# Half-width output matmuls in the first attention, and one probability tile normalised on the scalar engine

## What is computed

```python
x = LN(x + attention0(x))   # 16 heads of 8, differential: a = softmax(q1 k1) - lam * softmax(q2 k2), no mask
x = LN(x + ffn0(x))         # 352 wide, fp4 quantised inputs and weights, silu gate
x = LN(x + attention1(x))   # 16 query heads of 64, 4 key heads, rotary, causal softmax
x = LN(x + ffn1(x))         # 8 experts of 512, top 1, relu
```

```python
w = softmax(where(causal, q @ k.T / 8, -1e30)); out = w @ v
```

## Time and profile before

| | |
|---|---|
| median of 3 runs | 1437.1 us (1436.81 to 1442.52) |
| profiled execution | 1440.72 us, span 1438.9 us |
| mean granted TensorE clock | 0.863 |
| TensorE / VectorE / ScalarE / GpSimd busy | 81% / 55% / 45% / 32% |
| L1225, output matmuls of the first attention | 1024 instructions, 164.5 us busy |
| L436, divisions on GpSimd | 256 instructions, 278.6 us busy |

### The profile page before, as it was taken

One profiled execution on the slowest core, in us unless ns is written; L12 is line 12 of the kernel. 1 busy time (PEld: TensorE's weight loads), 2 busy tenths in 40 slices (PEclk: granted clock), 3 DMA queues, 4 the chain that ended last, 5 costly groups with the idle time before them and its releaser, 6 DMA issues. The chain is left out here.

```text
span 1438.9 us, 18598 instructions
## 1 busy us (share of the span) xinstructions
PE 1171.1 (81%) x6601; PEld 562.6 (39%) x6601; DVE 796.9 (55%) x1852; ACT 646.9 (45%) x1456; POOL 466.6 (32%) x495
## 2 busy tenths in 40 slices
PE   2699745888987769899987769899987698999686
PEld 1112221222454424344454424344454465455454
DVE  4677346772875566563875466563775411765212
ACT  1166512665364226666364226666364233165132
POOL 2000024000898040000898040000887020598000
PEclk7578855979998679999998669999998799999799
DMA  5600030000030000000030000000000000000000
GB/s 144 171 2 1 9 95 1 2 1 9 1 92 6 0 1 1 2 2 15 1 91 6 1 1 1 2 2 8 1 1 1 1 1 1 8 1 1 1 1 8
DMA packets 30923, 24.93 MB, mean 17 GB/s; under 512 B 12328, under 2 KB 27760, under 8 KB 30064
## 3 DMA queue, kind: packets, MB, share of 16 engines
q1 hardware_dynamic: 30832, 23.75, 6.5%
HBM read 16.01 MB, written 7.34 MB: 16 GB/s over the span
## 5 line engine op out<-in xcount | busy, mean ns | idle before, releaser
L717 DVE TENSOR_REDUCE mx<-ps 128x1 f32<-128x512 f32 x512 | 324.2, 684 | 173.0 <-PE ps L1203 171.3
L981 ACT ACTIVATE PROB<-ps 128x512 f32<-128x512 f32 x512 | 274.2, 603 | 206.4 <-PE ps L1194 205.4
L436 POOL TENSOR_SCALAR PROB<-PROB,rsum 128x128 f32<-128x128 f32 (+3 forms) x256 | 278.6, 1105 | 18.1 <-DVE rsum L857 18.0
L1023 ACT ACTIVATE PROB<-ps,mx 128x128 f32<-128x128 f32 (+3 forms) x256 | 132.7, 524 | 162.0 <-DVE mx L852 161.3
L1203 PE MATMUL ps<-kst,qst 24*128 24x512 bf16 x512 | 157.4, 456 | 39.8 <-DVE mx L717 26.6
L945 ACT ACTIVATE MREG<-ps,b_sb 128x512 f32<-128x512 f32 x128 | 88.1, 689 | 179.9 <-PE ps L1131 179.3
L1225 PE MATMUL ps<-PROB,v 128*32 128x512 f32 x1024 | 164.5, 723 | 4.2 <-ACT OREG L990 2.4
L1131 PE MATMUL ps<-xnT,w_sb 128*128 128x512 f32 x256 | 148.0, 680 | 10.1 <-DVE MREG L662 5.6
L1194 PE MATMUL ps<-qst,kst 27*128 27x512 bf16 x512 | 131.0, 417 | 28.8 <-ACT PROB L981 17.6
L1283 PE MATMUL ps<-cst,PROB 128*128 128x128 f32 x640 | 111.6, 296 | 46.1 <-POOL PROB L436 25.3
L417 POOL CAST mparts<-mx 128x16 bf16<-128x16 f32 x32 | 6.3, 196 | 439.1 <-DVE mx L717 439.1
(11 more groups left out here) (182 smaller groups left out, 1317.0 us busy)
## 6 DMA issues: line engine op xcount, KB each, us to landing
qk_terms<-RREG SPq DMA_DIRECT2D x48, 128.0 KB, 2.1
kst<-qk_terms SPq DMA_DIRECT2D x16, 192.0 KB
qst<-qk_terms SPq DMA_DIRECT2D x16, 192.0 KB
w_sb<-in_L_ffn_W_dram SPq DMA_DIRECT2D x1, 2048.0 KB
qst<-mrow SPq DMA_DIRECT2D x96, 4.0 KB
ZC<-in_L_attn_x_dram SPq DMA_DIRECT2D x4, 256.0 KB, 2.9
XN<-in_L_attn_x_dram SPq DMA_DIRECT2D x4, 256.0 KB, 7.9
out_dram<-XP SPq DMA_DIRECT2D x4, 256.0 KB, 2.3
```

Source lines behind the costliest of these rows:

```text
L436: pool.tensor_scalar(tile, tile, rsum1[:, 2 * v + half:2 * v + half + 1], None, ALU.mult).then_inc(scaled1, 1)
L717: dve.tensor_reduce(mx0[:, ga % 2, col:col + 1], ps[:, max_banks[MAX_SLOT[n] % len(max_banks)], :], AX, ALU.max, negate=True).then_inc(slo ...
L981: act.activation(prob0[:, s % 2, q % 4, q % 8 // 4], ps[:, s0_banks[q % len(s0_banks)], :], ACT.Exp, scale=float(HD0) ** -0.5).then_inc(ex ...
L1023: act.activation(prob1[:, half, at:at + w], ps[:, a1_bank(v, half), 0:w], ACT.Exp, bias=mx1[:, col:col + 1], accum_out=sum1[:, col:col + 1 ...
```

## The change

The output matmuls of a step are cut into halves of 256 query columns. A step m has four parts u = 0 to 3 (half of the keys u // 2, half of the queries u % 2). A table AV_PARTS places them: u = 0, 1, 2 in quarters 1, 2 and 3 of step m + 1, u = 3 in quarter 0 of step m + 2 when m is even and in quarter 3 of step m + 1 when m is odd. `av0_done` now counts two a step, and ScalarE waits for it in quarters 0 and 2. In the second attention the second head's tile of width 512 (v % 4 = 3) is multiplied by its reciprocal on ScalarE, in place, by `scale_last`, which is placed after the exponentials of tile v + 1 and ahead of the copy of a turned tile; GpSimd keeps the other seven tiles of a pair. TensorE waits on a semaphore of its own for it.

```diff
--- before.py
+++ after.py
@@ -74,6 +74,12 @@
 HID_KEEP = {(3, 1): 0, (4, 1): 1, (5, 1): 2, (6, 1): 3}
 DOWN = {(3, 2): 0, (4, 2): 1, (5, 2): 2, (6, 2): 3}
 DOWN_KEEP = {(3, 3): 0, (4, 3): 1, (5, 3): 2, (6, 3): 3}
+
+
+AV_PARTS = {}
+for _m in range(16):
+    for _u, _at in enumerate(((_m + 1, 1), (_m + 1, 2), (_m + 1, 3), (_m + 2, 0) if _m % 2 == 0 else (_m + 1, 3))):
+        AV_PARTS.setdefault(_at, []).append((_m, _u))
 O0_TURN = {(9, 0): 0, (9, 2): 1, (10, 0): 2, (10, 2): 3, (11, 3): 4, (13, 3): 5, (15, 3): 6, (17, 3): 7}
 O0_OUT = {(2 * g + 3, 0): g for g in range(NG)}
 UP = {(2 * e - 1, f): (e, f) for e in range(NE) for f in range(4)}
@@ -261,7 +267,8 @@
 
         proj1, v1_ready, rope_ready, qk_ready = sem("proj1"), sem("v1_ready"), sem("rope_ready"), sem("qk_ready")
         a1_ready, max1_done, exp1_done, rcp1_ready = sem("a1_ready"), sem("max1_done"), sem("exp1_done"), sem("rcp1_ready")
-        scaled1, turned1, kept1_dve, kept1_act = sem("scaled1"), sem("turned1"), sem("kept1_dve"), sem("kept1_act")
+        scaled1, scaled1_act = sem("scaled1"), sem("scaled1_act")
+        turned1, kept1_dve, kept1_act = sem("turned1"), sem("kept1_dve"), sem("kept1_act")
         av1_done, oT_ready = sem("av1_done"), sem("oT_ready")
         y1_ready, att1_sum, bo_added = sem("y1_ready"), sem("att1_sum"), sem("bo_added")
 
@@ -340,7 +347,7 @@
 
             def load_terms(k):
                 if k:
-                    sp.wait_ge(av0_done, 16 * k)
+                    sp.wait_ge(av0_done, 32 * k)
                 for c, dst in ((1, kst), (0, qst)):
                     for j in range(HF):
                         src = terms_dram[c].rearrange("t d j g n -> j (t d) g n")[j]
@@ -431,7 +438,7 @@
 
                 pool.wait_ge(rcp1_ready, NV * r + v + 1)
                 w = P * (v % 4 + 1)
-                for half in range(2):
+                for half in range(1 if v % 4 == 3 else 2):
                     tile = prob1[:, half, P * (v % 4) * (v % 4 + 1) // 2:][:, 0:w]
                     pool.tensor_scalar(tile, tile, rsum1[:, 2 * v + half:2 * v + half + 1], None, ALU.mult).then_inc(scaled1, 1)
 
@@ -972,8 +979,8 @@
                 for s, c in STEPS:
                     if k < BATCH:
                         if 0 <= s < 16:
-                            if c == 0 and s >= 2:
-                                act.wait_ge(av0_done, 16 * k + s - 1)
+                            if c in (0, 2) and s >= 2:
+                                act.wait_ge(av0_done, 32 * k + 2 * (s - 2) + 1 + c // 2)
                             if c == 0 and s == 0 and k >= 2:
                                 act.wait_ge(av1_done, 8 * (k - 1))
                             for q in (8 * s + 2 * c, 8 * s + 2 * c + 1):
@@ -982,7 +989,7 @@
                                                scale=float(HD0) ** -0.5).then_inc(exp0_done, 1)
                         if (s, c) in O0_OUT:
                             g = O0_OUT[s, c]
-                            act.wait_ge(av0_done, 16 * k + 2 * (g + 1))
+                            act.wait_ge(av0_done, 32 * k + 4 * (g + 1))
                             if g >= 4:
                                 act.wait_ge(o0_turned, NG * k + g - 3)
                             elif k:
@@ -1023,6 +1030,12 @@
                         act.activation(prob1[:, half, at:at + w], ps[:, a1_bank(v, half), 0:w], ACT.Exp, bias=mx1[:, col:col + 1],
                                        accum_out=sum1[:, col:col + 1]).then_inc(exp1_done, 1)
 
+                def scale_last(v):
+
+                    act.wait_ge(rcp1_ready, NV * r + v + 1)
+                    tile = prob1[:, 1, 6 * P:10 * P]
+                    act.activation(tile, tile, ACT.Copy, scale=rsum1[:, 2 * v + 1:2 * v + 2]).then_inc(scaled1_act, 1)
+
                 def keep_turned(u):
 
                     w, qt = pair_of(u), u % 4
@@ -1038,12 +1051,16 @@
                     return
                 for v in range(V_FIRST):
                     probabilities(v)
+                    if v == 4:
+                        scale_last(3)
                     if v == V_FIRST - 2:
                         for u in range(V_FIRST - TURN_LAG):
                             keep_turned(u)
                 for v in range(V_FIRST, V_END):
                     if v < NV:
                         probabilities(v)
+                    if v > 4 and v % 4 == 0 and v <= NV:
+                        scale_last(v - 1)
                     if v - TURN_LAG < NV:
                         keep_turned(v - TURN_LAG)
                     turn(k, nx, v)
@@ -1212,19 +1229,19 @@
                     if 0 <= i < BATCH:
                         experts_stream(s, c, i)
                     if k < BATCH:
-                        m = s - 1
-                        if 0 <= m < 16 and c in (1, 2):
-                            if c == 1:
+                        for m, u in AV_PARTS.get((s, c), ()):
+                            if u == 0:
                                 pe.wait_ge(exp0_done, 128 * k + 8 * (m + 1))
                                 if m == 0:
                                     pe.wait_ge(v0_ready, k + 1)
                                 if m % 2 == 0 and m >= 2:
                                     pe.wait_ge(o0_out, NG * k + m // 2)
-                            kt = 2 * (m % 2) + c - 1
+                            kt, qs = 2 * (m % 2) + u // 2, slice(256 * (u % 2), 256 * (u % 2) + 256)
                             for j in range(HF):
-                                ins = pe.matmul(ps[32 * j:32 * j + 32, 4, :], v0[:, kt, 4 * j + m // 4, :],
-                                                prob0[:, m % 2, j, c - 1, :], start=(kt == 0), stop=(kt == 3))
-                            if c == 2:
+                                ins = pe.matmul(ps[32 * j:32 * j + 32, 4, qs], v0[:, kt, 4 * j + m // 4, :],
+                                                prob0[:, m % 2, j, u // 2, qs],
+                                                start=(m % 2 == 0 and u == 0), stop=(m % 2 == 1 and u == 3))
+                            if u % 2 == 1:
                                 ins.then_inc(av0_done, 1)
                         if (s, c) in O0_TURN:
                             g = O0_TURN[s, c]
@@ -1276,7 +1293,10 @@
                     if u == 0:
                         pe.wait_ge(rope_ready, 24 * (r + 1))
                     for i, kept in enumerate((kept1_dve, kept1_act)):
-                        pe.wait_ge(scaled1, 2 * (NV * r + u) + i + 1)
+                        if i == 1 and qt == 3:
+                            pe.wait_ge(scaled1_act, 8 * r + u // 4 + 1)
+                        else:
+                            pe.wait_ge(scaled1, 7 * (8 * r + u // 4) + 2 * qt + i + 1)
                         if u:
                             pe.wait_ge(kept, NV * r + u)
                         for kt in range(qt + 1):
```

## The result

The changed kernel takes 1421.6 us (median of four runs, 1410.5 to 1422.7) against 1437.6 for the kernel before on the same chip; the ratio is 0.987, 95% interval 0.982 to 0.991, so 19 us with an interval of 12 to 26 (the two medians alone lie 16 apart). Predicted were 1417 and a range of 1400 to 1434. Its profiled execution has a span of 1420.3 us. Executions of one and the same program differ by 10 us here: in E0's series 1409.8 us went with a mean granted clock of 0.882 and 1421.6 with 0.867, and the traces show short stretches of the low clock in different places. Ratios are taken over the executions of a series and not from the medians, and where a few us matter I compare stretches of the traces.

What follows compares the result with a forecast made beforehand. TensorE was taken to bound the expert overlaps, TensorE and VectorE by turns the light ones, while GpSimd's divisions delay TensorE in second attention. Terms -15 + 4 - 9 = -20 us took 1437 to 1417; range 1400 to 1434.

Steps and rivals of the forecast that it cites:

- The light overlaps: Overlaps without experts, batches 0 and 1: evened output matmuls save 8 and 7 us, -15 in all, ends 0 and -30.
- The granted clock alternates in this stretch; I assume that this goes on: Light overlaps: clock keeps switching between 1.2 GHz (0.50) and 2.4 GHz (1.00), giving a mean quarter of 1.4 us.
- the sign of being wrong: First overlap: the forecast is wrong if its mean clock moves by more than 0.05 either way.
- The mechanism of evening: Light overlaps: spreading half sets over quarters bound by TensorE and by VectorE brings steps to 6.1 us on average, against 6.8.
- rival (c): Light overlaps: clock stays up once TensorE's work is even, quarters of 1.25 us, -30 instead of -15, total 1402; chance 0.15.
- The expert overlaps: Overlaps of batches 2 and 3: TensorE is the bound, net +1.8 us each, +4 in all, ends 0 and +8.
- 0.44 us per two steps: Output matmuls: two steps cost 4.44 us after against 4.0 before, 3.5 us for each expert overlap.
- 0.35 of each transpose's wait: Expert overlaps, odd steps: 0.35 us of TensorE's 1.20 wait for VectorE goes; five such steps, 1.75 us.
- The divisions: Second attention: 32 of 256 GpSimd divisions go to ScalarE, -9 us, between -4 and -13.
- The clean pair: Round 3 head pair of 8.91 us: the wait removed and the wait made are both 0.43 us, 0.0 a pair.
- the pair with the table loads: Second attention, rounds 0 to 2: TensorE's 1.31 us wait behind two table loads; 0.2 us a round gained in the middle.
- That same wait also swallows the 0.56: Rounds 0 to 2: the 1.31 us wait for ScalarE after two table loads absorbs 0.56 us given back at GpSimd's wait.

Runs made afterwards that it cites:

- E0: The changed kernel measured once more in a later series, against the kernel before: 1415.3 us, ratio 0.983.
- B1: Changed kernel with whole sets in the expert overlaps and the scaled copy behind the turned copy: 1409.3 us, ratio 0.980 against the kernel before.
- E3: Kernel before with all output matmul sets halved, both halves together in old quarters 1 and 2, divisions on GpSimd: ratio 0.9998.
- E8: Kernel before with whole sets in quarters 1 and 3 instead of 1 and 2, divisions on GpSimd: 1460.0 us, ratio 1.014.
- E9: E8 with each maxima matmul of quarters 0 and 2 issued twice in the light overlaps: 1464.4 us, ratio 1.017 against the kernel before.
- E2: Kernel before with only the 32 divisions moved to ScalarE, output matmuls whole in quarters 1 and 2: 1431.8 us, ratio 0.996.
- E6: Changed kernel with tile 11, ahead of the two table loads, divided on GpSimd again: 1412.6 us, ratio 0.981 against the kernel before.

## Why the prediction came out

The total was right, the three terms less so: 6 us too little gain in the light overlaps, 2 too little cost in the expert ones, 3 to 6 too much gain in the second attention. That these nearly cancelled was luck.

**The light overlaps (-15 forecast, -21 measured; -20 to -30 over seven traces with the same instructions there).** The step that failed is "The granted clock alternates in this stretch; I assume that this goes on". It did not: the clock stood at 1.00 for 48 us, and the mean over the 16 score steps went from 0.77 to 0.85 (0.92 in E0), more than the 0.05 that I had named as the sign of being wrong (on the longer stretch of the earlier trace rows it is 0.78 and 0.82, within the 0.05). The mechanism of evening was right: with the clock still mixed it takes 1.94 us off two steps, which then last 11.90 where I took 5.6 + 6.6 = 12.2. At the full clock a half set and a score quarter leave VectorE as the bound, and its ten maxima run without a pause:

```profile
109.00 6.23 DVE L724 TENSOR_REDUCE mx<-ps 128x1 f32<-128x512 f32 x10 [0.71 <-PE ps L1220]
```

There steps take 4.95 and 5.95 us. That is rival (c), the clock staying up, and in the two best traces it gave what the rival said (-29.6 in E0, -28.9 in B1). Halving alone brings 0 (E3), and spreading without halving left the clock down (E8). Where the clock is nearly or just the same, the order is worth 1.94 us in steps 3 and 4 and 1.12 in steps 9 to 12; the clock is worth 0.98 and 2.65 there. So the -21 is the forecast's evening and, on top, a clock that I had taken as fixed. I had given (c) 0.15, with an argument (shorter pauses) that E9 speaks against, though the outcome was as it said. Two slips in the sums did no harm. The stretch of 109.2 us runs beyond the 16 score steps, which took 103.8 or 6.5 each, not 6.8; but steps 2 to 8 took 6.9 on average. And 6 x 0.57 + 1.00 is 4.42, not 4.44.

**The expert overlaps (+4 forecast, +6 measured).** Here two errors nearly cancelled. I charged the 0.44 us per two steps everywhere, as if TensorE were the bound in every quarter. The steps themselves got no longer: 145.1 us for 16 in the fourth overlap, against 145.7 before. Odd steps, 10.30 us before, take 9.90; even ones, 9.05, take 9.32. In the kernel before TensorE stood short in the quarter after a light one, which I had not read:

```profile
570.64 0.66 PE L1203 MATMUL ps<-kst,qst 24*128 24x512 bf16 x2
570.91 0.09 PEld L1203 LDWEIGHTS ps<-kst,qst 24*128 24x128 bf16 x1 [0.18 <-DVE mx L717]
```

The second maxima load waits for VectorE and the quarter's matmuls take 0.74 us (570.49 to 571.23) instead of 0.33; after, that quarter starts later and takes 0.33. What I had put down as coming back, 0.35 of each transpose's wait, did not: that wait is 1.33 and 1.34 where it was 1.20. The cost is in two places that I did not price. Behind the last scores the sets of steps 14 and 15 stand with nothing beside them; that tail is 17.1 to 18.7 us where it was 14.9, part of it at the low clock (650.00 to 656.80 below). And in some executions low stretches of 3.4 us, 41 us apart, add 2.7 us:

```profile
530.50:533.90 3.40, 2.06 (x12) 0.66 (x15) 2.69 (x8) 2.58 (x7) 0.00 (x0) 1.00 0.02 5
533.90:537.30 3.40, 3.40 (x19) 1.99 (x20) 1.29 (x2) 1.77 (x3) 0.00 (x0) 0.50 0.02 4
...
858.30:861.70 3.40, 2.06 (x12) 0.74 (x15) 2.62 (x8) 2.55 (x8) 0.00 (x0) 1.00 0.00 0
861.70:865.10 3.40, 3.40 (x33) 1.37 (x25) 1.29 (x2) 2.41 (x4) 0.00 (x0) 1.00 0.02 4
...
650.00:656.80 6.80, 6.80 (x48) 2.22 (x44) 3.96 (x16) 3.91 (x7) 0.00 (x0) 0.50 0.01 2
```

The same instructions, with TensorE busy 2.06 of 3.40 us ahead in both, are followed by 0.50 in the third overlap and by 1.00 in the fourth.

**The divisions (-9 forecast; -6.3 in E2, interval -4 to -9; -3.3 in the changed kernel's trace).** The prize was read rightly: not 1.56 us a pair, but the wait in front of TensorE. From the first score load of the last pair to the last transpose of round 0 is 16.5 us where it was 18.7, the 2.2 of the forecast. The clean pair, forecast at 0.0, costs 0.36: the scaled copy is 0.72 instead of 0.68, the first wait 0.58 instead of 0.43, and the second wait, behind the 512-wide turned copy, is one that I had missed. Three such pairs in round 3 are 1.1 us, while the pair with the bias addition gave 0.88 (10.15 to 9.27). And in rounds 0 to 2 the pair with the table loads, forecast at -0.2, is 1.2 to 1.7 longer wherever the clock fell there (1.64 in the changed kernel's trace). "That same wait also swallows the 0.56" was right for the time and wrong for the clock: a wait swallowed by a later one makes that later one longer.

**Two sizes.** The scaled copy measured 720 ns (eight in round 3), against my 682 from the nearest row. The Trainium skill (ScalarE: Activation LUTs, What ACT_TABLE_LOAD costs) gave an estimate of 706 ns. The half set measured 0.57 us, as forecast. The Trainium skill (TensorE: Matmul & The Clock Gate, Part 3, What overlaps and what doesn't), with the page's own figure for a load, would have put an estimated 0.21 us of loads in the open, an estimated 0.64 us a half set, so here the trace does not agree.

## What to carry to other kernels

Give each step between two engines that share few buffers the same work, and look at it at both levels of the clock: the same evening was worth 20 to 30 us in two overlaps where VectorE could then run through (the higher clock that came with it included), and cost 5 to 6 where TensorE was the bound. When an operation is moved to another engine's queue, the prize is the wait in front of the bound engine, and the price is every copy behind it in the new queue; putting it one place later gave back 0.56 us a pair. When one wait goes and the next swallows it, the next pause grows: here from 1.31 to 1.69 us, and in 16 of 21 cases the clock fell with it, at 1.2 to 1.7 us, more than the 0.56 of the wait. Before a gain is put down to an order or to the clock, look for stretches of the traces with the same instructions at two levels.

## What the runs showed of the hardware

- TensorE busy 47.75 of 48 us did not lift the granted clock from 0.50 (E9), and a pause that is 0.37 us longer (1.69 against 1.32 in E6) went with a fall to 0.51 for 3.4 us in the 16 matmuls behind it, 4.02 us instead of 2.37, while with one of 1.68 us in E0 the clock stayed. Busy time in the trace does not by itself tell which level is granted.
- Equal instructions in two stages of one execution had the clock fall in one and not in the other; executions of one program lay between 1409.8 us (mean clock 0.882) and 1421.6 (0.867). A difference below some 5 us is better read in the stages of the traces than in the medians.
- The same instructions in four steps took 26.04 us at a granted clock of 0.87 and 23.39 at 1.00.
- Four-column-group fp32 sets of 256 columns take 0.57 us, of 512 columns 1.00 us, and two halves together 1.00: the second entry right behind the first costs nothing (E3, ratio 0.9998, with 256 halves in pairs).
- GpSimd's 512-wide division takes 1.56 us, the same on ScalarE 0.72.
